# A third tile for the gated activations of a feed-forward layer, and the split into high and low parts moved one tile back

## What is computed

```python
x = x + attn(layernorm(x))
x = x + xattn(layernorm(x), ctx_1024)
x = x + ffn(layernorm(x))

def ffn(x):                     # x: 8 x 512 x 256, hidden size 1024
    h = silu(x @ w1.T * s1) * (x @ w2.T * s2)
    h = gelu(h @ h1.T * h1s)
    h = gelu(h @ h2.T * h2s)
    return h @ w3.T * w3s
```

## Time and profile before

| | us |
|---|---|
| median of 3 runs | 1571.29 |
| lowest and highest of them | 1568.92 and 1574.66 |
| the profiled execution | 1573.35 |
| its span, first to last instruction | 1571.6 |
| PE busy in the span | 1516.3 (96%) |
| DVE, ACT, POOL busy | 1088.5, 956.2, 493.0 |
| mean granted clock of PE | 0.985 |

### The profile page before, as it was taken

One profiled execution on the slowest core, in us unless ns is written; L12 is line 12 of the kernel. 1 busy time (PEld: TensorE's weight loads), 2 busy tenths in 40 slices (PEclk: granted clock), 3 DMA queues, 4 the chain that ended last, 5 costly groups with the idle time before them and its releaser, 6 DMA issues.

```text
span 1571.6 us, 29271 instructions
## 1 busy us (share of the span) xinstructions
PE 1516.3 (96%) x10780; PEld 1283.6 (82%) x10780; DVE 1088.5 (69%) x2727; ACT 956.2 (61%) x2246; POOL 493.0 (31%) x798
## 2 busy tenths in 40 slices
PE   8999999999999999999976999999999899999998
PEld 6888888888888888888865887788888688888887
DVE  7999989999999999998995455644452534433432
ACT  6878887888888888887876445344533442222222
POOL 1554455445544554445541101010100101111210
PEclk9999999999999999999997999999999899999999
DMA  4000000000000000000133231331113332232221
GB/s 148 2 2 21 8 2 28 2 28 2 2 28 1 28 1 2 25 25 14 35 99 106 94 108 68 121 117 65 48 68 129 130 104 82 87 97 85 83 82 41
DMA packets 55770, 87.17 MB, mean 55 GB/s; under 512 B 4160, under 2 KB 33216, under 8 KB 55616
## 3 DMA queue, kind: packets, MB, share of 16 engines
q1 hardware_dynamic: 55616, 85.10, 16.1%
HBM read 55.72 MB, written 29.36 MB: 54 GB/s over the span
## 4 chain that ended last, share of the span: by engine, by line
PE 81%; DVE 8%; issue 4%; ACT 3%; DMA 2%; POOL 2%; SPq 0%; POOLq 0%; DVEq 0%; ACTq 0%
PE bank L969 14%; PE bank L971 12%; PE bank L623 10%; PE bank L543 9%; PE bank L595 8%; PE bank L545 7%; PE bank L544 7%; PE bank L607 6%; DVE gt L1357 2%; PE bank L975 2%; DVE Hb L1233 2%; ACT Hb L1108 1%; PE bank L1091 1%; PE bank L1100 1%; DMA pf<-h_scratch 1%
## 5 line engine op out<-in xcount | busy, mean ns | idle before, releaser
L809 POOL TENSOR_SCALAR P<-P,stats 128x512 f32<-128x512 f32 (+3 forms) x512 | 269.7, 548 | 362.7 <-DVE stats L787 362.5
L682 ACT ACTIVATE P<-P,stats 128x512 f32<-128x512 f32 (+3 forms) x512 | 283.5, 560 | 19.2 <-DVE stats L779 18.5
L646 ACT ACTIVATE PT<-bank 128x512 fp32r<-128x512 f32 (+1 forms) x384 | 184.7, 524 | 82.5 <-PE bank L607 81.0
L1233 DVE TENSOR_TENSOR Hb<-gt,Hb 128x512 fp32r<-128x512 f32 x128 | 91.6, 716 | 205.4 <-ACT Hb L1108 187.2
L969 PE MATMUL bank<-Hb,hw 128*128 128x512 f32 x512 | 209.2, 409 | 25.6 <-DVE Hb L1233 15.1
L779 DVE CUSTOM_DVE_ANT_0 P<-bank,cmask 128x256 f32<-128x256 f32 (+3 forms) x512 | 228.6, 483 | 1.0 <-issue 0.4
L696 DVE TENSOR_TENSOR PT<-bank,PT 128x512 fp32r<-128x512 f32 (+1 forms) x384 | 218.6, 594 | 5.5 <-ACT PT L646 3.9
L969 PE MATMUL bank<-w,hw 128*128 128x512 f32 x512 | 201.0, 393 | 4.3 <-DVE w L1233 3.5
L971 PE MATMUL bank<-Hb,hw 128*128 128x512 f32 x448 | 179.8, 401 | 0.0
L623 PEld LDWEIGHTS bank<-PT,V 128*128 128x128 f32 x1024 | 164.7, 189 | 17.9 <-DVE PT L696 1.1
L623 PE MATMUL bank<-PT,V 128*128 128x512 f32 (+3 forms) x1024 | 175.3, 318 | 1.2 <-DVE PT L696 0.8
(11 more groups left out here) (217 smaller groups left out, 3278.0 us busy)
## 6 DMA issues: line engine op xcount, KB each, us to landing
h_scratch<-go SPq DMA_DIRECT2D x64, 256.0 KB, 2.1
xs<-x_scratch SPq DMA_DIRECT2D x23, 512.0 KB, 4.0
qf<-h_scratch SPq DMA_DIRECT2D x32, 256.0 KB, 4.0
pf<-h_scratch SPq DMA_DIRECT2D x32, 256.0 KB, 4.9
stageA<-in_h SPq DMA_DIRECT2D x14, 512.0 KB, 3.6
x_scratch<-x SPq DMA_DIRECT2D x8, 512.0 KB, 3.1
x_scratch<-xs SPq DMA_DIRECT2D x8, 512.0 KB, 3.0
out<-xns SPq DMA_DIRECT2D x16, 256.0 KB, 2.2
```

The costliest lines, as they stand in the source:

```text
L646: return e.activation(dst, src, ACT.Copy, scale=scale)
L682: e.activation(p, p, ACT.Exp, bias=st_[:, k:k + 1], scale=-1.0, accum_out=st_[:, 8 + k:9 + k]).then_inc(s_exp, 1)
L809: e.tensor_scalar(p, p, stats[P % 4][:, k:k + 1], 1.0, ALU.mult, ALU.mult).then_inc(s_norm, 1)
L1233: return e.tensor_tensor(dst, x, y.bitcast(f32), ALU.subtract)
```

## The change

The tiles gt become three. The new one lies in SBUF where bias rows of the cross-attention lay before, so the first `silu` that writes it (n = 2) waits for their last readers. `silu` of tile n now waits for `hl` of tile n - 3. And for b = 1 to 7 the steps `hh` and `hl` of tile m - 1 stand behind `hm` of tile m, with those of tile 7 at the end. The hand-written list of batch 0 stays as it is. The numbers of instructions do not change, nor do PE's, POOL's and SP's lists.

```diff
         if b:
+
             for m in range(8):
-                o += [(k, b, m) for k in ("g", "u", "silu", "hm", "hh", "hl")] + also(b, ("w", m))
+                o += [(k, b, m) for k in ("g", "u", "silu", "hm")]
+                if m:
+                    o += [("hh", b, m - 1), ("hl", b, m - 1)]
                 if b == B - 1 and m in (3, 5):
                     o.append(("w3", m // 2 - 1))
+            o += [("hh", b, 7), ("hl", b, 7)] + also(b, ("w", 7))
...
-    gt = [at(L + 196 + 2 * i, f"gt{i}", [128, 512]) for i in range(2)]
+    gt = [at(L + k, f"gt{i}", [128, 512]) for i, k in enumerate((196, 198, 46))]
...
-                w.wait_ge(s_hlo, n - 1)
+                w.wait_ge(s_hlo, n - 2)
+                if n == 2:
+                    w.wait_ge(s_xvf, 4)
+                    w.wait_ge(s_bqlo, 1)
...
-                e.activation(gt[n % 2][:, :], bank["g", b, m][:, :], ACT.Silu,
+                e.activation(gt[n % 3][:, :], bank["g", b, m][:, :], ACT.Silu,
                              scale=s1c[:, 0, m:m + 1]).then_inc(s_silu, 1)
...
-                copy(Hb[m][:, 0, :], gt[n % 2][:, :]).then_inc(s_hhi[1], 1)
+                copy(Hb[m][:, 0, :], gt[n % 3][:, :]).then_inc(s_hhi[1], 1)
...
-                g = gt[n % 2]
+                g = gt[n % 3]
...
-                g = gt[(8 * b + m) % 2]
+                g = gt[(8 * b + m) % 3]
...
-                e.tensor_scalar(Hb[m][:, 0, :], gt[n % 2][:, :], 1.0, 1.0, ALU.mult, ALU.mult).then_inc(s_hhi[0], 1)
+                e.tensor_scalar(Hb[m][:, 0, :], gt[n % 3][:, :], 1.0, 1.0, ALU.mult, ALU.mult).then_inc(s_hhi[0], 1)
```

## The result

The changed kernel takes 1549.1 us (median of six runs, 1546.91 to 1553.2) against 1571.23 for the kernel before in six runs beside it. The ratio is 0.9859, with a 95% interval of 0.984 to 0.9877: 22.1 us less, about 19 to 25. Forecast were 23.0 us less and a time of 1548.3.

A forecast was written before the change was run, and what follows sets the result against it. PE, busy 96% of the span, was taken to lose time waiting for late low parts (`hl`) and at a lowered clock. Gains of 14.6 us (batches 1 to 6) plus 8.4 (batch 7) took 1571.3 to 1548.3 us; range 1545.5 to 1556.

The forecast's parts named there:

- Throughput: Gate stages: with `hh` overlapped, DVE needs 1.40 us per tile and ACT 1.32, both below PE's 1.81.
- The end of the batch: Batches 1 to 6: last `hm` at +14.7, last `hl` done +16.9, needed +18.6; whole loss of 14.6 us goes.
- What is late next: Second layer, batches 1 to 6: no new PE waits, since other engines' work there starts from PE's results.
- Contention: `hl` on DVE beside POOL's copy: each meeting costs DVE 0.39 us, 0.8 us per batch in batches 1 to 6.
- Batch 7: Tile 0 of `h` still waits 2.3 us (1.1 to 3.1); gain 8.4 us, best 9.6, worst 5.2.
- The clock: PE's clock fall behind waits costs about 1.9 us in batches 2 and 3 each, 2.4 in batch 7; none assumed after.
- The total: Whole kernel: 14.6 + 8.4 = 23.0 us gained, from 1571.3 to 1548.3 us.
- A: Last batch keeps its loss through POOL, w3 splits and clock: gain there 2 to 5 us, time 1553 us; chance 0.17.
- B: Gate stages: pace stays between 1.81 and 2.09 us per tile, about half gained, 1559 us; chance 0.07.
- C: No change: PE would only wait in the second layer for cross-attention or layer norm, 1571 us; chance 0.04.
- D: Slower: POOL's copy beside DVE makes a tile 2.3 us, clock falls in all seven batches, 1590 us; chance 0.02.

The follow-up runs named there:

- the first two experiments: Against the kernel before: third gt tile with the old step order, 1573.25 us; then new step order with two gt tiles, 1564.35 us.
- copy and w3: Kernel before, with tile 0's high part of batch 7 copied by ACT instead of POOL and both w3 splits behind tile 7: 1564.65 us, ratio 0.9964.
- the copy alone: Kernel before, with only the high part of tile 0 of batch 7 copied by ACT instead of POOL: 1568.79 us, ratio 0.9991.
- batch 7 alone: Changed kernel with three gt tiles, but the new step order only in the last batch: 1562.27 us, ratio 0.9953 against the kernel before.

## Why the prediction was right, step by step

*Throughput, right.* DVE is no longer the slower one: it is idle 0.46 us per tile behind PE. The work of one tile, which I had put at 1.40 us, is shorter still: from 1209.36 to 1210.02 `hm` takes 0.66 us to the start of the next instruction, and `hl` takes 0.60 where nothing waits, 1.26 together. For `hm` I had taken the row's duration, 0.75, but the next instruction begins before its recorded end.

*The end of the batch, right.* +14.71 and +16.9, as worked out. The sum over batches 1 to 6 was 14.6 us, and the profiles show 14.74. The cover of twelve to fourteen matmuls was enough in all six. That the tile and the order are both needed is shown by the first two experiments: alone they give nothing and 7 us.

*What is late next, right.* Nothing. No new wait appeared; the only wait for a low part that is left is the 0.28 us in batch 7.

*Contention, wrong in its place.* I charged DVE 0.39 us for each `hl` beside POOL, 0.8 us per batch. The durations of `Hb` in the changed kernel, by DVE and POOL (line, engine, operation, count, least/median/greatest ns):

```profile
L1240 DVE TENSOR_TENSOR Hb<-gt,Hb x128: 676/692/1092, 840.0 to 1534.0; 128x512 fp32r<-128x512 f32 x128
...
L1455 POOL TENSOR_SCALAR Hb<-gt x24: 614/988/1526, 837.6 to 1205.3; 128x512 fp32r<-128x512 f32 x24
```

POOL's copy took 0.99 us in the median where it took 0.62 before, and DVE's `hl` stayed at 0.69. All fourteen copies of batches 1 to 7 that started behind an `hl` took 0.985 to 0.997 us. In the timeline of batch 1 above, `hl` had begun at 904.05, 0.17 us before the copy at 904.22; the copy became longer and `hl` took its usual 0.68. The charge was paid by POOL, which had the time. With these copies on ACT the median of `hl` is the same, 692 ns. Only in batch 7, where POOL's copies for the third layer were already under way, the last two low parts took 2.04 us together. The Trainium skill, page "GPSIMD Engine Reference", section Specifications, says that POOL shares its SBUF interfaces with DVE and contends with DVE instructions that have two SBUF inputs. The rows agree, and add that the sharing may slow either. They also answer what the prediction had to leave open: beside `hm`, which reads one of its tensors from PSUM, neither was slowed. POOL's first copy of batches 1 to 6 ran beside an `hm` alone, and it took 0.62 us each time and `hm` 0.74 to 0.75 (897.96 and 897.11 in the timeline of batch 1).

*Batch 7, right in kind and mis-sized.* The term was a wait of 2.3 us (1.1 to 3.1), and it was 0.28, outside the term's own bounds; the gain was 10.25 us, above the 9.6 that I had called the best. Its terms, one by one. `hl` of tile 0 started at +6.22 and not at +6.97, 0.75 us. This is no part of the change: from the start of POOL's flag reduction to its first copy of batch 7 lie 7.93 us in the trace of before, 7.18 after, and 7.1 to 7.9 in six more traces of kernels with either order. Then DVE's chain of eight `hl`, six `hm` and two splits: I had 12.2 us by durations, and by starts (0.60, 0.66, 1.14) it is 11.0. And the meetings with POOL: the last two `hl` lasted 2.04 us where they would take 1.28 alone, 0.76 us for my 1.2. Together about 2.2 us earlier, done at 1210.02 + 2.04 = +18.1. PE, which also came to `h` 0.24 us sooner (+14.51), stood ready at +17.9. The third tile of `h` began at +22.4, where I had named 24 to 25 us. PE waited once, briefly, and the clock stayed at 1.00, as assumed.

*The clock, right in kind and a little mis-sized.* The working put 1.9 us of the loss of each of batches 2 and 3 down to the clock and 2.4 in batch 7. It was 1.6 in batches 2 and 3, by the spare matmuls and by the two equal batches of the kernel with the order alone. The 1.9 came from taking the waits, 1.1 us longer, for the lateness; the starts of `hm` in the earlier trace rows give 4.40 - 2.99 = 1.4 us, which leaves 1.6 of the 3.0. In batch 7 it was about 2.8, since matmuls of tile 0 ran at half clock too, where the 2.4 counted tile 1 alone.

*The total, partly luck.* The forecast of 23.0 us is closer to the measured 22.1 than its parts were. The stages of the two profiles give 25.0, and the 1.9 us by which batch 7 was put too low happen to stand against the 2.9 us by which the medians show less than the stages.

*The rivals.* A (batch 7 keeps its loss) and B (half of the pace) did not come. C and D neither. The run with the order alone shows how D could have come: at 2.24 us per tile the pace was indeed slower than before, and still the kernel was faster, since fewer steps of it stood on the path. My price of 7 x 1.6 us for such a pace counted eight steps where six are on the path, and the clock fell in two batches of that kernel, not in seven.

*What stays open.* The stages of the profiles gain 0.5 to 3 us more than the medians in every experiment with a gain (8.2 and 5.9 with copy and w3, 3.1 and 1.4 with the copy alone, 9.8 and 9.3 with batch 7 alone). About 0.5 us of it is the trace of before, whose batch 7 is that much longer than in the two other traces that have it. For the rest no run gives a cause. In two measurements the stages' gain lies outside the interval of the times: with copy and w3 (3.6 to 7.7), and in the second measurement of the change, 25.1 us by the stages against 19.2 to 23.7.

## What to carry to other kernels

In a chain over several engines, put the pace of each engine per tile, waiting included, beside the pace of the engine that is to be kept busy; a step that another engine does between two of one's own is to be moved behind the next tile's, and that may take a buffer more. Here the buffer alone gave nothing and the order alone 7 us of 22, so try the two together before giving one up. Where PE's granted clock falls behind a wait, the wait costs more than it lasts, and here even spare matmuls won part of that back.

## What the runs showed of the hardware

- Of a copy on POOL and a subtraction on DVE with both inputs in SBUF that overlapped, the one that started second was slowed: POOL's 128x512 copy took 0.62 us alone and 0.99 when `hl` was running (fourteen times in the changed kernel), DVE's `hl` 0.69 alone and 1.08 when the copy was running. Beside `hm`, with one tensor in SBUF and one in PSUM, the copy kept its 0.62 and `hm` its 0.75.
- PE's granted clock went to half behind waits of 2.2 us in batches 2 and 3 of before, and stayed at full behind 1.1 us (batches 1 and 4 to 6), and behind 2.1 us in two pieces in batch 7 of the kernel with the copy and w3 moved. Behind one wait of 1.50 us it fell in batch 2 of the kernel with the order alone and stayed at full in batch 3, and the fall cost 1.6 us. With spare matmuls in the waits of before it stayed at full.
- On DVE, in the packed stretch looked at, an instruction begins 0.08 us before the recorded end of the one ahead of it: in batch 7 of the changed kernel the next starts 0.66 us after an `hm` of 0.74, 0.60 after an `hl` of 0.68, 1.14 after a split of 1.22. A sum of durations overstates such a packed chain by 7 to 13%.
- POOL's first copy behind its flag reduction came 7.1 to 7.9 us after the reduction's start in batch 7 of eight traces, in either order of the steps. Why it varies is open.
